# Softmax divided before its transposes, values stationary in row and column tiles, half of each norm on ScalarE

## The reference

```python
def norm(x, t, gw, gb, bw, bb):           # t is the condition
    g = (t @ gw.T + gb)[:, None, :]
    b = (t @ bw.T + bb)[:, None, :]
    return g * x * rsqrt(mean(x * x, -1) + 1e-6) + b

def attention(x, Wq, Wk, Wv, Wo):         # 16 heads of 16 channels
    attn = einsum('blhd,bmhd->bhlm', q, k) / 4
    o = einsum('bhlm,bmhd->blhd', softmax(attn), v)
    return o @ Wo.T

x1 = x + attention(norm(x, ...1), ...)
y  = x1 + (silu(n2 @ gate_w.T) * (n2 @ hid_w.T)) @ out_w.T    # n2 = norm(x1, ...2), 1024 hidden
out = x + y
```

## Time and profile before

| | |
|---|---|
| three runs | 1078.95 us median (1076.10 to 1081.28) |
| profiled execution | 1077.67 us, span 1075.9 us |
| granted PE clock, mean | 0.992 |
| PE busy / DVE / ACT / POOL | 1032.2 / 673.7 / 423.5 / 339.5 us |
| first matmul of scores, tile 0 / tile 1 | 29.86 / 79.41 us |
| first matmul of the MLP alone (iteration 16) | 1033.79 us |

### The profile page before, as it was taken

The page is one execution under the profiler, slowest core; times in us unless marked ns, Lnnn a source line. Parts: engine busy times, 40 slices in busy tenths (PEclk is TensorE's granted clock), DMA queues, the critical chain, the costliest instruction groups (busy, mean ns, idle before and its releaser), DMA issues.

```text
span 1075.9 us, 22083 instructions
## 1 busy us (share of the span) xinstructions
PE 1032.2 (96%) x8240; PEld 919.7 (85%) x8240; DVE 673.7 (63%) x1306; ACT 423.5 (39%) x903; POOL 339.5 (32%) x284
## 2 busy tenths in 40 slices
PE   6879999999999999999999999999999999999987
PEld 5768889889888988988888888988988898898876
DVE  4645766566666656766666676657666665666543
ACT  3433343444334343343434434344433434334232
POOL 4313233232333223233232323323233323324142
PEclk9979999999999999999999999999999999999999
DMA  4100000010100001010010100001010000100000
GB/s 169 41 1 21 2 24 18 1 39 0 39 0 19 19 0 39 0 39 0 0 39 0 39 0 25 14 0 39 0 39 0 19 19 0 39 0 21 1 21 19
DMA packets 18968, 21.67 MB, mean 20 GB/s; under 512 B 640, under 2 KB 18240, under 8 KB 18816
## 3 DMA queue, kind: packets, MB, share of 16 engines
q1 hardware_dynamic: 18720, 21.24, 5.9%
q10 hardware_dynamic: 224, 0.10, 0.0%
HBM read 12.95 MB, written 8.39 MB: 20 GB/s over the span
## 4 chain that ended last, share of the span: by engine, by line
PE 67%; issue 23%; POOL 5%; ACT 2%; DVE 2%; DMA 0%; POOLq 0%; ACTq 0%; DVEq 0%; SPq 0%
PE ps L824 8%; PE ps L737 6%; PE ps L809 6%; PE ps L739 6%; PE ps L738 5%; PE ps L817 5%; PE ps L832 4%; PE ps L842 4%; PE ps L845 4%; PE ps L835 4%; PE ps L843 4%; PE ps L833 4%; POOL h_lo L247 4%; PE ps L744 1%; PE ps L853 1%
## 5 line engine op out<-in xcount | busy, mean ns | idle before, releaser
L247 POOL TENSOR_TENSOR h_lo<-shared,h_hi 128x512 fp32r<-128x512 f32 x128 | 164.7, 1286 | 360.5 <-ACT h_hi L371 313.3
L577 DVE SCALAR_TENSOR_TENSOR shared<-shared,ps 128x512 f32<-128x512 f32 x128 | 87.8, 686 | 128.1 <-ACT shared L366 127.6
L737 PE MATMUL ps<-out_w_hi,h_hi 128*128 128x256 f32 x512 | 154.1, 301 | 9.5 <-POOL h_lo L247 9.5
L366 ACT ACTIVATE shared<-ps 128x512 f32<-128x512 f32 x128 | 76.4, 597 | 194.1 <-PE ps L835 125.2
L739 PE MATMUL ps<-out_w_hi,h_lo 128*128 128x256 f32 x512 | 144.4, 282 | 0.0
L738 PE MATMUL ps<-out_w_lo,h_hi 128*128 128x256 f32 x512 | 143.7, 281 | 0.0
L824 PEld LDWEIGHTS ps<-values,probsT 128*128 128x128 f32 x1024 | 129.8, 192 | 13.2 <-ACT probsT L376 8.0
L376 ACT ACTIVATE probsT<-ps 128x512 f32<-128x512 f32 x128 | 74.7, 597 | 163.8 <-PE ps L817 163.8
L824 PE MATMUL ps<-values,probsT 128*128 128x66 f32 x1024 | 130.8, 271 | 4.0 <-ACT probsT L376 4.0
L371 ACT CAST h_hi<-shared 128x512 fp32r<-128x512 f32 x128 | 78.9, 616 | 99.7 <-DVE shared L584 99.7
L563 DVE TENSOR_REDUCE row_max<-ps 128x8 f32<-128x512 f32 x128 | 87.8, 686 | 37.7 <-PE ps L809 36.7
(11 more groups left out here) (101 smaller groups left out, 2150.9 us busy)
## 6 DMA issues: line engine op xcount, KB each, us to landing
x_in<-in_x SPq DMA_DIRECT2D x16, 512.0 KB, 3.4
out<-result SPq DMA_DIRECT2D x15, 512.0 KB, 2.9
shared<-in_attT SPq DMA_DIRECT2D x1, 1024.0 KB, 7.0
shared<-in_gateT SPq DMA_DIRECT2D x1, 1024.0 KB, 8.9
shared<-in_hidT SPq DMA_DIRECT2D x1, 1024.0 KB, 4.8
shared<-in_outT SPq DMA_DIRECT2D x1, 1024.0 KB, 5.5
out<-result SPq DMA_DIRECT2D x2, 256.0 KB, 2.2
result<-in_modT SPq DMA_DIRECT2D x1, 256.0 KB, 4.7
```

What stands on the lines that cost most here:

```text
L247: nc.gpsimd.tensor_tensor(h_lo[:, j % 2, :], h[:, :], h_hi[:, j % 2, :].bitcast(F32), ALU.subtract).then_inc(h_lo_done, 1)
L737: nc.tensor.matmul(dst, a_hi, b_hi, start=first, stop=False, skip_group_check=skip)
```

## The change

**Softmax.** DVE writes the shifted scores into `probs`, ACT's exp works there in place, DVE sums each row of each sequence and takes reciprocals, and POOL multiplies (`divide`). Only then does PE transpose (`transpose_probs`), and ACT copies from PSUM to `probsT` (`keep_transposed`). `probs`, `probsT`, `row_max` and `recip` have four slots in place of two. The columns of ones and the zeros in `values` go.

**Product with the values.** After four pairs, `values_probs(t, r)` makes 32 products of 64 rows and 32 stationary columns: the values of one sequence and pair are stationary, `probsT` of that sequence moves with 128 columns, on row tiles of 64 and column tiles of 32. The result is channel-major. ACT (`first_heads`) and DVE (`second_heads`) take each head's own columns from it into `attT`, then it is split in high and low; `attention_channels` goes. `scores(t, 1)` waits for `attT_done`.

**Norms.** The second channel half goes to ACT (`second_norm`, eight ACTIVATEs of 64 columns with scale and bias from `mod`), the first stays on DVE. For the second norm POOL subtracts the first half's low part, DVE (`low_norm2`) the second's. The first chunk of the MLP loses its special order (`first_chunk_high`, `first_chunk_low`).

**MLP.** `h` has two slots, `h_hi` and `h_lo` four (`KEPT`). `gate` waits for `silu_done` of the chunk before, `hid` for `h_done`.

**Orders.** All four engines' orders are written anew.

```diff
 # gpsimd
+            def divide(t, p):
+                pool.wait_ge(recip_done, PAIRS * t + p + 1)
+                own = probs[:, p % TOGETHER, :].rearrange("p (b k) -> p b k", k=L)
+                nc.gpsimd.tensor_tensor(own, own, recip[:, p % TOGETHER, :].unsqueeze(2).to_broadcast([P, SEQS, L]),
+                                        ALU.mult).then_inc(divided, 1)
...
                 if mlp:
                     low_hidden(t - 1, 0)
+                    low_hidden(t - 1, 1)
+                if attend:
+                    divide(t, 0)
+                if mlp:
                     sum_of_inputs(t - 1)
-                    low_hidden(t - 1, 1)
                     low_hidden(t - 1, 2)
+                if attend:
+                    divide(t, 1)
+                if mlp:
+                    low_hidden(t - 1, 3)
+                if attend:
+                    divide(t, 2)
                 if ahead:
                     inverse_rms(t + 1, ms1, ms1_done, mse1, mse1_done, inv1, inv1_done, scaled1)
+                if attend:
+                    divide(t, 3)
...
+                if attend:
+                    divide(t, 4)
                 if mlp:
                     low_hidden(t - 1, 6)
                 if attend:
+                    divide(t, 5)
+                    divide(t, 6)
+                    divide(t, 7)
+                if mlp:
+                    low_hidden(t - 1, 7)
+                if attend:
                     inverse_rms(t, ms2, ms2_done, mse2, mse2_done, inv2, inv2_done, scaled2)
 # scalar
+            def second_norm(u, m, src, transposed, read, xn, done):
+
+                act.wait_ge(transposed, CH * u + CH)
+                wait(act, read[0], read[1])
+                for b in range(SEQS):
+                    tok = slice(b * L, (b + 1) * L)
+                    last = nc.scalar.activation(xn[:, 1, tok], src[:, tok], ACT.Identity,
+                                                bias=mod[:, m + 1, 1, bass.ds(u * SEQS + b, 1)],
+                                                scale=mod[:, m, 1, bass.ds(u * SEQS + b, 1)])
+                last.then_inc(done, 1)
...
+            def keep_transposed(t, p):
+                act.wait_ge(probsT_mm, PAIRS * t + p + 1)
+                wait(act, pv_mm, ROUNDS * t + p // TOGETHER)
+                nc.scalar.copy(probsT[:, p % TOGETHER, :], ps[:, bank_of(p), :]).then_inc(probsT_done, 1)
 # vector
+            def reciprocals(t, p):
+                dve.wait_ge(exp_done, PAIRS * t + p + 1)
+                nc.vector.tensor_reduce(sums[:, p % TOGETHER, :],
+                                        probs[:, p % TOGETHER, :].rearrange("p (b k) -> p b k", k=L),
+                                        AX_X, ALU.add).then_inc(summed, 1)
+                dve.wait_ge(summed, PAIRS * t + p + 1)
+                wait(dve, divided, PAIRS * t + p - TOGETHER + 1)
+                nc.vector.reciprocal(recip[:, p % TOGETHER, :], sums[:, p % TOGETHER, :]).then_inc(recip_done, 1)
 # tensor
+            def transpose_probs(t, p):
+                pe.wait_ge(divided, PAIRS * t + p + 1)
...
+            def values_probs(t, r):
+
                 for k in range(BLK):
+                    tok = slice(k * P, (k + 1) * P)
+                    for seq in range(2):
+                        rows = slice(seq * L, seq * L + L)
+                        for g in range(TOGETHER):
+                            chans = slice((TOGETHER * r + g) * ROWS, (TOGETHER * r + g + 1) * ROWS)
+                            last = nc.tensor.matmul(ps[g * ROWS:(g + 1) * ROWS, PAIR + 2 * r + seq, tok],
+                                                    values[rows, k, chans], probsT[rows, g, tok],
+                                                    start=True, stop=True)
                 last.then_inc(pv_mm, 1)
```

More of the change, by code:

```diff
@@ L101, in conditioned_block @@
         keys = sb("keys", [P, CH, TOK])
[L102 to L107, removed]
+        values = sb("values", [P, BLK, D])
+        row_max = sb("row_max", [P, TOGETHER, SEQS])
+        probs = sb("probs", [P, TOGETHER, TOK])
+        sums = sb("sums", [P, TOGETHER, SEQS])
+        recip = sb("recip", [P, TOGETHER, SEQS])
+        probsT = sb("probsT", [P, TOGETHER, TOK])
+        attT = sb("attT_sum", [P, TOK])
         attT_hi = sb("attT_hi", [P, 2, TOK], F32R)
@@ L388, in _ @@
             first_queries(0)
-            for half in range(2):
-                even_values(0, half)
+            first_values(0)
             def scale_second(t):
@@ L425, in iteration @@
                     tanh(t - 1, 1)
+                    high_hidden(t - 1, 1)
                 if alone(t):
                     high_weights(2, hid_w_in, 16, hid_w_hi[:, :, :].rearrange("p c n -> p (c n)"), 0)
+                if mlp:
+                    tanh(t - 1, 2)
                 if attend:
-                    exp(t, 2)
-                if mlp:
-                    high_hidden(t - 1, 1)
-                if attend and not alone(t):
-                    keep_input(t)
+                    exp(t, 1)
+                    keep_transposed(t, 0)
                 if alone(t):
@@ L436, in iteration @@
                 if mlp:
-                    tanh(t - 1, 2)
+                    high_hidden(t - 1, 2)
+                if attend:
+                    exp(t, 2)
+                if attend and not alone(t):
+                    keep_input(t)
+                if mlp:
+                    tanh(t - 1, 3)
+                if attend:
+                    keep_transposed(t, 1)
+                if mlp:
+                    high_hidden(t - 1, 3)
                 if attend:
                     exp(t, 3)
-                if mlp:
-                    high_hidden(t - 1, 2)
-                    tanh(t - 1, 3)
-                    high_hidden(t - 1, 3)
                 if alone(t):
@@ L619, in _ @@
             second_queries(0)
-            for half in range(2):
-                odd_values(0, half)
+            second_values(0)
             def maxima_and_shift(t, p):
@@ L678, in iteration @@
                 if attend:
-                    divide(t, 2)
+                    shift(t, 2)
+                    reciprocals(t, 1)
+                    row_maxima(t, 3)
                 if mlp:
@@ L901, in _ @@
             pe.wait_ge(w_split, 1)
-            project_k(0)
+            for c in range(CH):
+                project_k(0, c)
             for c in range(CH):
```

581 lines of the change are left out of this document (282 added, 299 removed).

## The result

The changed kernel takes 1236.08 us, the median of four runs (1233.61 to 1240.87), against 1077.74 us for the kernel before beside it (four runs, 1076.1 to 1081.28): ratio 1.1457, interval 1.1433 to 1.1482, 158 us more. The prediction said 1230. The profiled execution has a span of 1231.4 us.

A forecast was written before the change was run, and what follows sets the result against it. PE's matmul stream, busy 96%, was taken as the bound. Steady tiles of 73.1 us against 63.9 gave 14 x 9.2 + 16 + 10 - 3.5 = +151, so 1229, stated as 1230 us; range 1140 to 1340.

The forecast's parts named there:

- Rival 5: The three divides reach PE in time, so 54 us go and the kernel gets faster: 1024 us; chance 0.05.
- rival 4: Part of the waits is absent, some 4 to 5 us per tile fewer: 1100 to 1165, say 1140 us; chance 0.12.
- `values_probs`: New product with the values on PE: 128 passes per tile at 30 ns, 3.9 us; upper bound 14 us.
- the three waits: PE waits for POOL's divide before `transpose_probs` 0, 1 and 2: 2.75 us each, 8.2 us per tile.
- the second half: Smaller PE waits around it, at `hid(6)`, `project_q(0)` and pairs 5 and 6 behind `divide`: 1.7 us per tile.
- Rival 3: Column tiles in `values_probs` do not overlap: half overlap 1278 us, none 1390 us; chance 0.12.
- The turn: Between tiles, PE waits 0.6 us for the scaled `x1` and 1.6 for `second_norm2`: 2.2 us per tile.
- Gate 0: Its low passes on PE wait for DVE's `low_norm2` behind `row_max` 0: 0.5 us per tile.
- gate 5: Its last pass on PE waits for `keep_transposed` 2 and 3 behind a cast: 0.8 us per tile.
- "Change no matmul": Regrouped `channel_major`, gate and hid order and four `h_hi`/`h_lo` buffers leave matmuls alone; PE work 59.5 us per tile.
- rival 2: The clock falls in half of the 45 waits, costing some 2 us each: 1280 to 1350, say 1310 us; chance 0.18.
- Ends: First tile 66 us for 49.5, +16; last tile, without `ahead`, +10; tail of MLP alone −3.5 us.

The follow-up runs named there:

- e5: Changed kernel with only POOL's order altered: divides 0, 1 and 2 ahead of the `low_hidden` each stood behind; 1195.2 us, ratio 1.1096.
- e2: Changed kernel with eight thrown-away 512-column matmuls on PE after each of `down` 0, 1 and 2, filling the waits for the divide; 1222.7 us, ratio 1.1348.
- e7: Changed kernel with every product of `values_probs` made twice, 128 more passes per tile; 1283.1 us, ratio 1.191.
- e6: Changed kernel with neighbouring products of `values_probs` alternating between the two halves of rows; 1235.7 us, ratio 1.1472.
- e8: Changed kernel with transposes of pairs 0 to 2 one gate and hid chunk later and both halves of the second norm on DVE; 1074.06 us, ratio 0.9964.
- e9: Changed kernel with late transposes, second norm on DVE, divide 3 ahead of `inverse_rms`, and first-tile `low_weights(2)` behind divide 3; 1070.87 us, ratio 0.9926.
- e1: Changed kernel with only PE's order altered: transposes of pairs 0, 1 and 2 one chunk of gate and hid later; 1109.4 us, ratio 1.0293.

## Why the prediction was right, and where it was not

**The cause is the forecast's.** The three transposes wait for a divide that comes late, behind a late `h_lo` on POOL and behind `hidden`, sum and reciprocal on VectorE. Three experiments take hold of it at different points: PE's order (−127 us), the divide itself (−126), POOL's order (−41). The gains are not to be added: they open the same wait. The prediction had both ways, with at least 6.0 us left when POOL's queue is free; e5 measured about 4.9. Rival 5 (the divides are in time) and rival 4 (part of the waits absent) fall by the 45 waits of 2.0 to 2.6 us.

**The sizes, per steady tile.** The sum of 73.1 met 73.2, but by errors that cancel. Measured: 7.2 + 1.95 + 0.4 + 0.9 + 0.4 us of waits, and 60.6 of matmuls, which is what these waits leave of e2's tile at the full clock (71.5), then 1.7 of clock. That the total hit so closely is therefore partly luck: 1.7 us too much for `values_probs`, 1.0 for the three waits and 1.5 for the second half stand against 2.8 too little for the other matmuls and 1.7 for the clock.
- The three waits: 7.2 us (2.25 + 2.58 + 2.40) for 8.2. The chain had its divide at 1.27 us; it took 1.05, below the lower bound of 1.2, 0.7 us for three. The remainder is mostly where a wait is counted from: the walk went from start to start, and the idle time in brackets begins at the recorded end of the last matmul, 0.16 us later.
- `values_probs`: 1.08 us for 64 passes with the step to the next group, so 2.2 us for 128, not 3.9. Rival 3 is refuted. e7's 14 ns a pass, times the eight tiles (two of rows, four of columns), is 0.11 us, the prediction's own price of a pass that overlaps with none: all eight overlap. e6 shows that the order of rows makes no difference. The Trainium skill ("TensorE: Matmul & The Clock Gate", Part 3: weight loads overlap running matmuls only where row groups differ) spoke for this rival; the runs here do not agree with it for this shape. Nor did the kernel before, whose matmuls use all 128 rows: there a load starts together with the matmul ahead of it (1067.13), and PE and PEld were busy 96% and 85% of the span.

```profile
1067.13 0.19 PEld L738 LDWEIGHTS ps<-out_w_lo,h_hi 128*128 128x128 f32 x1
```

- The turn: 0.56 + 1.39 = 1.95 for 2.2, by `second_norm2` in 2.48 us for 2.7 (below).
- Gate 0 0.37 for 0.5, gate 5 0.86 for 0.8, the second half 0.44 for 1.7: there only one wait of the four is left, the one of 0.44 for `divide`.
- "Change no matmul" was too short. In a steady tile of e8, which runs at the full clock, the matmuls without their listed waits take 59.8 us (62.4 less 0.56, 0.37, 1.27 and 0.41). The prediction's sum with the 2.2 put in gives 63.1 − 6.7 − 0.8 + 2.2 = 57.8. Behind passes of 512 and 256 columns, whose usual distances are 0.23 and 0.118 us, the next start is more than 0.04 us late at 29 places of a tile of e8, 3.4 us in all, and at 17 places before, 1.6 us (waits over 0.25 us left out). These are small gaps at the edges of groups, which the list of waits does not name; some 1.9 us more of them is the term that was missing. What each of them waits for was not tried. In the changed kernel itself the same difference gives 60.6, with the 0.16 us at the start of each wait in it.
- The clock: missing from the forecast, and the part of rival 2 that came true. The prediction itself had named a granted clock under 1.00 in the steady tiles as a sign of being wrong. Summed over the run, (1 − clock) comes to 53 us in the changed kernel, to 9 before. Tiles 2 to 14 have 19 stretches of some 3.4 us. By the periods, against 71.46 us without any, one behind a divide's wait costs 1.5 us (tiles of 72.95) and one at the turn 0.7 (tiles of 72.15; the waits behind it get shorter there, the first divide's 2.0 for 2.2): 1.7 us a tile on the average, some 25 us in all. Rival 2 asked for stretches behind half of the 45 waits and some 80 us; it was 11 of 39 in these tiles, and a third of the time.
- Four slips of the working, none of which decides: 4.26 less 1.42 is 2.84 and not 2.75; the turn's 5.1 less 4.3 is 0.8 and not 0.6; rival 4's 4 to 5 us a tile would be 1155 to 1170 and not 1100 to 1165; and "no row here has it" in rival 3 passes over the loads of the kernel before.

**Ends.** To the second tile +15.1, for +16; of it 2.6 us is a later start of the first scores (32.5 for 29.9), which lies between 28 and 33 us in the profiles of these kernels whatever their order, so the first tile is 62.0 us, not 66. The wait there has the cause given: `divide(0)` behind `low_weights(2)`.

```profile
38.51 4.50 POOL L263 TENSOR_TENSOR hid_w_lo<-shared,hid_w_hi 128x2048 fp32r<-128x2048 f32 x1 [11.07 <-ACT hid_w_hi L339]
42.97 2.04 POOL L256 TENSOR_TENSOR probs<-probs,recip 128x512 f32<-128x512 f32 x2
```

```profile
44.06 1.12 PE L882 MATMUL ps<-consts_sb,probs 128*128 128x128 f32 x4 [8.44 <-POOL probs L256]
```

Last tile and tail: +12.7 for +6.5. Up to the first matmul of the MLP alone (1192.05 for 1033.79) the last tile gave +15.4 (forecast 10), with waits of 2.5, 1.7 and 2.0 us in its second half and at the turn and one of 1.26 for the cast of `xn_hi`; the tail gave −2.8 (forecast −3.5).

**What the change was worth.** PE's saving is real: 62.4 us a steady tile in e8 against 63.8. It comes to 0.4 to 0.7% of the kernel once its consumers stand late enough in the order. That is less than the 54 us of rival 5, by those small gaps (1.9 us a tile), the remaining waits (2.6 us a tile in e8 for 0.8 before), and the 13 us or so more that the first tile still takes. Why e9's first tile did not gain more is known only as far as its waits: a shorter one at the transposes, a new one at the scores, and a clock that was low from 55 to 75 us.

## What to carry to other kernels

When an operation moves ahead of its consumer on another engine's queue, follow that queue: here transposes placed right behind a chain of `hidden`, sum or `h_lo`, and a 1.05 us divide, cost 127 us, and one chunk's shift in PE's order took it back without touching the work. There can be two ways to the same wait: putting the divide first on POOL opened only the shorter part, because VectorE's way was 0.7 us behind. Walk every such wait as chain minus cover, term by term, and then ask for two things that a walk leaves out: the clock, which here fell behind some waits of 2 us and more and behind a pair of 0.56 and 1.39, and the small gaps at each new edge between groups of matmuls. A filled wait tells the clock's part of a wait from the wait itself, but look at every stretch: here the filling changed the clock in other places too.

## What the runs showed of the hardware

- Products of 64 rows, 32 stationary columns and 128 moving columns, in eight row and column tiles, start 14 ns apart on the average (e7; 17 ns when the step to the next group is counted to 64 of them), though each of these matmuls is recorded with 269 ns and its weight load with 106 (medians of the group below). A pass of 128 columns on the whole array, as in the transposes of the kernel before (L817), starts 0.11 us behind the one ahead. The order over rows changes nothing (e6).

```profile
L898 PEld LDWEIGHTS ps<-probsT,values x2048: 102/106/173, 54.8 to 1174.7; 64*32 64x32 f32 x187
L898 PE MATMUL ps<-probsT,values x2048: 269/269/418, 54.8 to 1174.9; 64*32 64x128 f32 x187
```

- Eight ACT instructions of 64 columns with scale and bias both from memory take 2.48 us in a row, a pitch of about 0.3 us each (414 ns for one); the estimate from the earlier trace rows was 0.33:

```profile
457.60 2.48 ACT L358 ACTIVATE shared<-ps,mod 128x64 f32<-128x64 f32 x8 [1.33 <-PE ps L813]
```

- The granted clock fell behind some waits of PE, and their length alone does not tell which. In tiles 2 to 14 of the changed kernel it fell behind 5 of 13 first waits (the five of 2.2 us; the others were 2.0), behind none of the second, which are the longest at 2.6, behind 6 of 13 third (2.4), and at 8 of 13 turns (0.56 and 1.39 us with a little work between). The same waits at the turn cost the clock in 12 of the last 14 tiles of e1 and in none of the tiles 2 to 9 of e2. The kernel before had waited up to 1.66 us at the full clock. Doubling `values_probs` (e7), which adds matmuls that fill few rows and columns and no idle time, brought more of these stretches: sum of (1 − clock) 88 us for 53. The trace does not say why.
- A 128x512 multiplication by a broadcast operand took POOL 1.05 us (mean of 128), less than the subtraction of the same size into fp32r, 1.30 (mean of 128).
